# Attention scores from stacked high and low parts through DRAM, and routing spread over more steps in another PSUM bank

## The reference

```python
# layer 0, attention: q from layernorm(x), k and v from ctx
scores = einsum('bhqd,bhkd->bhqk', q, k) / sqrt(16)
out = einsum('bhqk,bhkd->bhqd', softmax(scores), v) @ W_O + b_O
x = x + tanh(g) * out
# layer 0, experts: top 2 of 8, relu, 256 -> 1024 -> 256, gates by softmax of the two
# layer 1, attention: the same with a causal mask and a key mask, no biases, no W_O
# layer 1, experts: top 2 of 8 by sparsemixer, silu(gate) * up, 256 -> 512 -> 256
```

## Time and profile before

| | |
|---|---|
| median of three runs | 1904.41 us (1901.04 to 1904.66) |
| the profiled execution | 1892.92 us |
| its span, first to last instruction | 1891.1 us |
| mean granted clock of TensorE | 0.920 of full |
| busy: PE, DVE, ACT, POOL | 88%, 64%, 63%, 42% |
| attention of layer 0, first to last transpose of probabilities | 47.2 to 453.4 us |
| experts of layer 0 | about 510 to 985 us |
| attention of layer 1, likewise | 1030.9 to 1428.0 us |
| experts of layer 1 | about 1485 to 1850 us |
| chain of work that ended last | PE 81%, DVE 8%, DMA 3%, issue 3%, POOL 2%, ACT 2% |

### The profile page before, as it was taken

The page is one execution under the profiler, slowest core; times in us unless marked ns, Lnnn a source line. Parts: engine busy times, 40 slices in busy tenths (PEclk is TensorE's granted clock), DMA queues, the critical chain, the costliest instruction groups (busy, mean ns, idle before and its releaser), DMA issues.

```text
span 1891.1 us, 36389 instructions
## 1 busy us (share of the span) xinstructions
PE 1672.7 (88%) x12444; PEld 1587.1 (84%) x12444; DVE 1210.5 (64%) x2859; ACT 1196.0 (63%) x2795; POOL 792.5 (42%) x877
## 2 busy tenths in 40 slices
PE   3999999998399999999975999999994599999990
PEld 2898888887399999999974998888884599999990
DVE  3465566654477777777756667767655566666655
ACT  2776566663188888888853766655562477777760
POOL 2123333323356666666652112323312366666650
PEclk9998899996599999999997999989896699999995
DMA  2112222112467777788742223322220577777758
GB/s 92 46 47 66 62 55 56 48 39 71 124 206 231 233 233 229 228 230 234 229 155 88 62 63 84 83 75 76 55 71 26 175 238 225 231 234 232 229 181 275
DMA packets 209513, 265.59 MB, mean 140 GB/s; under 512 B 28224, under 2 KB 155460, under 8 KB 209200
## 3 DMA queue, kind: packets, MB, share of 16 engines
q1 hardware_dynamic: 189840, 222.36, 40.8%
q0 software_dynamic: 13632, 35.13, 5.1%
q10 hardware_dynamic: 5856, 5.77, 1.0%
HBM read 202.89 MB, written 45.69 MB: 131 GB/s over the span
## 4 chain that ended last, share of the span: by engine, by line
PE 81%; DVE 8%; DMA 3%; issue 3%; POOL 2%; ACT 2%; SPq 1%; POOLq 0%; DVEq 0%; ACTq 0%
PE ps L363 19%; PE ps L365 19%; PE ps L364 19%; PE ps L484 10%; PE ps L383 6%; PE ps L494 2%; PE ps L465 2%; POOL xs_scr L1132 2%; PE ps L399 1%; DMA U<-ys_scr 1%; PE ps L415 1%; PE ps L458 1%; DVE X L1331 1%; DVE mx L912 1%; DMA xs_scr<-U,PI 1%
## 5 line engine op out<-in xcount | busy, mean ns | idle before, releaser
L1035 POOL TENSOR_TENSOR KXR<-U,KXR 128x1024 fp32r<-128x1024 f32 (+1 forms) x156 | 334.4, 2144 | 308.0 <-ACT KXR L645 307.2
L363 PE MATMUL ps<-QR,KXR 128*128 128x256 f32 x1248 | 355.1, 285 | 8.5 <-DVE QR L1039 8.5
L364 PE MATMUL ps<-QR,KXR 128*128 128x256 f32 x1248 | 354.7, 284 | 0.0
L365 PE MATMUL ps<-QR,KXR 128*128 128x256 f32 x1248 | 354.3, 284 | 0.0
L645 ACT ACTIVATE KXR<-U 128x1024 fp32r<-128x1024 f32 (+1 forms) x312 | 287.7, 949 | 78.0 <-PE ps L365 62.1
L555 ACT ACTIVATE U<-ps,mx 128x128 f32<-128x128 f32 x1024 | 293.9, 388 | 4.7 <-DVE mx L912 4.7
L484 PEld LDWEIGHTS ps<-VA,U 128*128 128x128 f32 x2048 | 275.8, 203 | 11.8 <-DVE U L901 1.2
L484 PE MATMUL ps<-VA,U 128*128 128x17 f32 x2048 | 264.7, 263 | 1.0 <-DVE U L901 1.0
L363 PEld LDWEIGHTS ps<-QR,KXR 128*128 128x128 f32 x1248 | 238.6, 191 | 9.7 <-DVE QR L1039 9.7
L364 PEld LDWEIGHTS ps<-QR,KXR 128*128 128x128 f32 x1248 | 238.6, 191 | 0.0
L365 PEld LDWEIGHTS ps<-QR,KXR 128*128 128x128 f32 x1248 | 238.3, 191 | 0.0
(11 more groups left out here) (190 smaller groups left out, 3949.2 us busy)
## 6 DMA issues: line engine op xcount, KB each, us to landing
U<-in_wpack SPq DMA_DIRECT2D x234, 512.0 KB, 4.1
U<-xs_scr SPq DMA_DIRECT2D x78, 257.0 KB, 4.4
U<-in_wpack SPq DMA_DIRECT2D x78, 256.0 KB, 3.6
KXR<-U SPq DMA_DIRECT2D x512, 32.0 KB, 2.0
U<-in_ctx_t SPq DMA_DIRECT2D x16, 512.0 KB, 4.1
U<-ys_scr SPq DMA_DIRECT2D x32, 256.0 KB, 3.0
U<-ys_scr SPq DMA_DIRECT2D x16, 512.0 KB, 10.2
XR<-in_L_ffn_b SPq DMA_DIRECT2D x39, 128.0 KB, 3.9
```

Source lines behind the costliest of these rows:

```text
L363: e.matmul(o, wh, xh, start=first, stop=False)
L364: e.matmul(o, wh, xl, start=False, stop=False)
L365: return e.matmul(o, wl, xh, start=False, stop=done)
L1035: e.tensor_tensor(w_cols(L, WL, n), w_raw(L, n), hi, ALU.subtract).then_inc(*l_w[n](L, i))
```

## The change

**Scores.** A pair of heads takes 32 rows, and three of them are stacked on 96 partitions: Q as high, low, high and K as high, high, low. One matmul over 96 rows gives all three products. With K's zeros kept only within a pair it has 256 columns for two heads, and a unit takes two of them (and two mask matmuls of 256 columns in layer 1). To stack, Q and K with their rests are written to a DRAM scratch (`qk_d`, 1 MB each per group) and read back for half a group at a time by nine transfers (`sp_stack`). `QR` becomes the stacked `QX`, two half groups deep, and `KX` likewise; both parts of Q and K of one group stand in `U1`.

**Order of projections.** XT, Q and K come a group earlier or closer together: `X0`, `Q0`, `K0`, `V0`. Layer norm, the loads of x and YL, and CT move ahead with them (a line of the diff each). The loop begins at -38.

**Routing** moves to bank `BK`, into more and closer steps; the rank matmuls' result is copied to `RK` at once (in `dve_rests`), and `dve_route` and `dve_rank2` fall into `dve_max`, `dve_index`, `dve_sel`, `dve_rank` and `dve_rows`. `ot` and `op` keep `BO_` for themselves.

**VectorE's order.** The maxima of unit `s + 3` come first in a step, ahead of `rec`, `ON` and the rests. Layer norm's and `XR`'s four batches are split over two steps.

```diff
-        self.lt = (self.e0 + 4, self.e0 + (6 if g < NG - 1 else 5))
-        self.e1 = self.e0 + (8 if g < NG - 2 else 7 if g < NG - 1 else 6)
-        self.d = (2, 4, 5) if g < NG - 2 else (1, 3, 4) if g < NG - 1 else (1, 2, 3)
+        late = g == NG - 1
+        self.lt = (self.e0 + 4, self.e0 + 5)
+        self.e1 = self.e0 + 6
+        (self.max, self.index, self.sel, self.gates, self.exp, self.gates2, self.rk, self.rank, self.rows, self.scatter) = (
+            self.e1 + k for k in ((1, 1, 1, 1, 1, 2, 2, 3, 3, 3) if late else (1, 2, 2, 3, 3, 4, 3, 4, 5, 6)))
-FIRST, LAST = -21, 146
+FIRST, LAST = -38, 147
+X0, Q0, K0, V0 = (-10, -9), (-8, -7), (-1, 0), (4, 11)
...
+        KX = KXR[:, :].rearrange("p (r c a n) -> p r c a n", r=2, c=8, a=2)
+        QX = QR[:, :].rearrange("p (r c n) -> p r c n", r=2, c=8)
...
                 if 0 <= s + 4 < NU:
-                    js = slice(j * 128, j * 128 + 128)
-                    kh, kl = (KX[:, b % 2, p, m, 4 * z:4 * z + 4, :].rearrange("p h k -> p (h k)") for p in range(2))
-                    ins = three(e, bank[:, :], (QR[:, g % 2, 0, m, js], QR[:, g % 2, 1, m, js]), (kh, kl), True, L == 0)
+                    js = slice((b % 2) * 128, (b % 2) * 128 + 128)
+                    for c in range(2):
+                        o, pk = bank[:, c * 256:(c + 1) * 256].rearrange("p (a k) -> p a k", a=2), 2 * (i % 4) + c
+                        ins = e.matmul(o, QX[0:96, r, pk, js], KX[0:96, r, pk, :, js], start=True, stop=L == 0)
+                        if L == 1:
+                            ins = e.matmul(o, IR[:, :], MK[:, g % 2, j:j + 1, :].to_broadcast([128, 2, 128]), start=False, stop=True)
...
+                if s == p.rk:
+                    w.wait_ge(*m_rk[k])
+                    e.tensor_copy(RK[:, :, 0:p.n], BK[:, 0:64].rearrange("p (z g e) -> p z g e", z=2, g=G)[:, :, 0:p.n]).then_inc(*v_rk(*k))
...
             for s in range(FIRST, LAST):
+                if 0 <= s + 3 < NU:
+                    i = s + 3
+                    w.wait_ge(*m_s[L, i])
+                    e.tensor_reduce(mx[:, i % 4], ...)
                 if (b := bat(s, 6)) is not None:
                 dve_rests(e, w, L, s - 1)
-                if 0 <= s + 3 < NU:
-                        if (g := grp(s, -3 + j)) is not None:
+                        if (g := grp(s, -19 + j)) is not None:
-                    if (g := grp(s, -2 + j)) is not None:
+                    if (g := grp(s, -18 + j)) is not None:
-                if (g := grp(s, 2)) is not None:
+                if (g := grp(s, -14)) is not None:
-                if (g := grp(s, 5)) is not None:
+                for n in range(2):
+                    if (g := grp(s, -12 + n)) is not None:
...
+        def sp_stack(e, w, L, h):
+            g, r, ns = h // 2, h % 2, slice((h % 2) * 256, (h % 2) * 256 + 256)
+            if h >= 2:
+                w.wait_ge(*m_s[L, 8 * (h - 2) + 7])
+            w.wait_ge(*d_qd[L, g])
+            for n in range(3):
+                src = qk_d[L][g, 0].rearrange("(c a) (z n) -> a z c n", c=8, z=2)[:, (0, 1, 0)[n], :, ns]
+                e.dma_start(QX[32 * n:32 * n + 32, r].bitcast(F32), src).then_inc(*d_q[r](L, h, n))
+            w.wait_ge(*d_kd[L, g])
+            for n in range(6):
+                q, a = n // 2, n % 2
+                src = qk_d[L][g, 1].rearrange("(c b a) (z n) -> b a z c n", c=8, b=2, z=2)[a, :, (0, 0, 1)[q], :, ns]
+                e.dma_start(KX[32 * q + 16 * a:32 * q + 16 * a + 16, r, :, a, :].bitcast(F32), src).then_inc(*d_k[r](L, h, n))
...
-                        if (g := grp(s, -5 + j)) is not None:
+                        if (g := grp(s, -21 + j)) is not None:
-                    for h in range(8):
-                        hs = slice(16 * h, 16 * h + 16)
-                        e.dma_start(KX[hs, v, :, :, h, :].rearrange("p z m k -> p (z m) k").bitcast(F32),
+                if (g := grp(s, Q0[1] + 1)) is not None:
+                    w.wait_ge(*v_q[L, g, 1])
+                    e.dma_start(qk_d[L][g, 0].rearrange("(m p) n -> p m n", m=2), U1[:, 2048:4096].rearrange("p (m n) -> p m n", m=2)).then_inc(*d_qd(L, g))
+                if (g := grp(s, K0[1] + 1)) is not None:
+                    w.wait_ge(*v_k[L, g, 1])
+                    e.dma_start(qk_d[L][g, 1].rearrange("(m p) n -> p m n", m=2), U1[:, 0:2048].rearrange("p (m n) -> p m n", m=2)).then_inc(*d_kd(L, g))
+                for n in range(2):
+                    if (g := grp(s, (3, 12)[n])) is not None:
+                        sp_stack(e, w, L, 2 * g + n)
```

More of the change, by code:

```diff
@@ L313, in w_raw, with uses_bk @@
             return U1[:, n * 1024:n * 1024 + NFs[L] * D // 2]
-        def bank7(L):
+        def uses_bk(L):
             out = []
             for s in range(FIRST, LAST):
[L319 to L324, removed]
+                for name, at, empty in (("xt", X0, v_xt), ("q", Q0, v_q), ("k", K0, v_k), ("v", V0, a_v)):
+                    for n in range(2):
+                        if (g := grp(s, at[n])) is not None:
+                            out.append(((name, g, n), empty[L, g, n]))
                 for p in PARTS:
@@ L975, in dve_attention @@
                             w.wait_ge(*a_ct[L, NG - 1])
-                        for j in range(p.lo, p.hi):
-                            ins = e.tensor_scalar(xr(p.g)[:, 0, j, 0:D], X[:, p.g * G + j], mv[:, 1, j, 0:1], rs[:, 1, 1, j:j + 1], ALU.subtract, ALU.mult)
-                        ins.then_inc(*v_xr(*k))
-                    if s == p.e1 + p.d[0]:
-                        dve_route(e, w, L, p)
+                        elif p.lo == 0 and p.g:
+                            w.wait_ge(*d_sc[(p.g - 1) % 2][L, p.g - 1, 0, 1, G - 1])
+                            w.wait_ge(*m_lt[L, p.g - 1, 0, 1])
+                        mid = (p.lo + p.hi) // 2
+                        for j in (range(p.lo, mid), range(mid, p.hi))[s - p.e0 - 2]:
+                            ins = e.tensor_scalar(xr(p.g)[:, 0, j, 0:D], X[:, p.g * G + j], mv[:, 1, j, 0:1], rs[:, 1, 1, j:j + 1], ALU.subtract, ALU.mult)
+                        if s == p.e0 + 3:
+                            ins.then_inc(*v_xr(*k))
+                    if s == p.max:
+                        dve_max(e, w, L, p)
+                    if s == p.index:
+                        dve_index(e, w, L, p)
+                    if s == p.sel:
+                        dve_sel(e, w, L, p)
+                    if s == p.gates:
                         dve_gates(e, w, L, p)
-                    if s == p.e1 + p.d[1]:
+                    if s == p.gates2:
                         dve_gates2(e, w, L, p)
-                    if s == p.e1 + p.d[2]:
-                        dve_rank2(e, w, L, p)
+                    if s == p.rank:
+                        dve_rank(e, w, L, p)
+                    if s == p.rows:
+                        dve_rows(e, w, L, p)
                 if (b := bat(s, 11)) is not None:
@@ L1215, in sp_attention @@
             for s in range(FIRST, LAST):
-                if (g := grp(s, -4)) is not None:
+                if (g := grp(s, -8)) is not None:
                     if g >= 2:
@@ L1224, in sp_attention @@
                                     .rearrange("p (b s) -> p b s", b=G)).then_inc(*d_mi(g))
-                if L == 0 and (g := grp(s, -8)) is not None and g:
+                if L == 0 and (g := grp(s, -22)) is not None and g:
                     sp_load_x(e, g)
```

278 lines of the change are left out of this document (131 added, 147 removed).

## The result

The changed kernel is a little slower: 1922.31 us median of 20 runs (1897.08 to 1932.76) against 1905.16 us for the kernel before (1900.40 to 1917.64), a ratio of 1.0058, 95% interval 1.0034 to 1.0082. Ratios here leave out the executions that fell in a slower state of the chip, so they are not the quotients of the medians. Later the same two kernels, run again, gave 1.0089 (1.0054 to 1.0125). I had forecast 1881 us, faster.

What follows compares the result with a forecast made beforehand. TensorE was taken to bound the attention groups. Steady-state savings of 71 us, +50 us before the first units and -2 us in layer 0's tail gave -23 us: 1881 us on the median's scale, range 1832 to 1926.

Steps and rivals of the forecast that it cites:

- Scores, 0.45 us a unit: Score matmuls of each unit: two of 256 columns instead of three of 512 save 0.45 us, bounds 0.13 to 0.54.
- Clock of layer 0's routing groups: Layer 0's four routing groups: mean clock 0.89 (before 0.93), 3 us idle each, 196 us against 214.8.
- the clock holds: Rival: routing groups at 0.95 with 2 us idle take 45.3 us, whole kernel 1831 us; chance 0.20.
- Clock of layer 1's routing groups: Layer 1's four routing groups: mean clock 0.90 (before 0.94), 4.5 us idle each, 200 us against 212.5.
- the formula: Group time: full-clock work divided by 1 - 0.465f, f being the share of time at low clock, plus idle time.
- Last groups: Last two groups of each layer: 84 us against 98.7 in layer 0, 81 against 94.2 in layer 1.
- DRAM round trip hidden in steady state: Q and K through DRAM: 6.4 us write plus 8.6 us half-group read fit within 27 us of lead.
- Start, layer 0: Before layer 0's first unit: more serial projections put first scores at 61.5 against 41.44 us; +18 us after 2 back.
- Layer 1 with the tail: Start of layer 1, +32 us from serial projections and YL additions, with layer 0's tail at 2 us less.
- Waits on PI gone: Layer 0's output projection no longer waits for a bank held until PI is written: 13.7 us over six waits.
- Maxima first costs nothing: VectorE's new order costs nothing by itself and keeps exponentials from waiting for value matmuls.
- the clock giving way: Rival: thin steps and new stalls put routing groups at 0.80 and 54.7 us, whole kernel 1928 us; chance 0.18.

Runs made afterwards that it cites:

- r_after: The changed kernel itself, unchanged, run again beside later runs: 1918.87 us, 1.0089 of the kernel before.
- r_e1: e1 once more, unchanged, on another chip: 1871.28 us, 0.9811 of the kernel before.
- e1: Changed kernel with YL's loads, additions and the bn_stats behind them four steps earlier in layer 1: 1875.38 us, 0.9860 of the kernel before.
- e4: Changed kernel with XT and Q of group 1 moved behind the first scores in both layers: 1907.54 us, 1.0021 of the kernel before.
- e13: e9 with the maxima back behind the reciprocals, ON and the rests, as in the kernel before: 1889.68 us, 0.9864 of the kernel before.
- e9: e1 with one added 480-column matmul ahead of each batch's router matmuls, both layers: 1852.50 us, 0.9713 of the kernel before; 0.9966 on a fourth chip.
- e3: Changed kernel with score matmuls issued three times over in each layer's last sixteen units: 1930.71 us, 1.0153 of the kernel before.
- e8: Changed kernel with e1's and e4's edits plus two added 512-column matmuls per step of each layer's last group: 1957.22 us, 1.0122 of the kernel before.

## Why the prediction was wrong, point by point

- **Scores, 0.45 us a unit**: right. With the clock at 1.00 a routing group of layer 0 of the changed kernel (r_after) was 42.40 us with 41.73 of TensorE work; I had 41.3.

```profile
202.69:245.09 42.40, 41.73 (x342) 39.68 (x342) 31.24 (x102) 33.69 (x96) 18.17 (x39) 1.00 0.72 175
```

- **Clock of layer 0's routing groups**: 0.89 forecast, 0.95 measured, and idle time 0.7 us a group, not 3. Four groups 177.5 instead of 196. Both terms were too dark here; in layer 0 it was the rival "the clock holds" (0.95, 45.3 us a group) that came out. The first two took 82.9 us (forecast 85.4), with one miss inside: the second of them now has a router step, so that its TensorE work is 41.33 us (r_e1, at full clock), not 38.3.
- **Clock of layer 1's routing groups, the step that failed**: 0.90 forecast, 0.79 measured. The idle time was about right (15.3 / 4 = 3.8 us against 4.5), and so was the formula: 41.3 / (1 - 0.465 x 0.42) + 3.8 = 55.1 us, measured 55.6. At 0.90 it gave 50. The four groups are 22.5 us over the forecast, all of it clock. The first two, put at 86, took 108.5; with the wait gone (e1) they take 82.5 and the four 198.2, which is what I had forecast (86 and 200). I had written that K's rest stands behind two additions, and priced it once, for the start. It stands there in each group, and I took its idle time, some 3 us, as the whole price: the 17 to 20 us at 0.50 behind it I had put at nothing.
- **Last groups**: forecast 84 and 81 us for the last two, measured 93.2 and 91.9. That is 9 and 11 us more. The clock did not dip, it stayed at 0.50 (in r_after, layer 0's last group had a mean of 0.80, and the last two took 76.3). The missing row was a plain step without projections at the low clock; none of the kernel before has one with thin scores. What decides whether the clock comes back there stays open.
- **DRAM round trip hidden in steady state**: right; no score matmul waited for `KX` or `QX` after the first unit. The landing times were 5.0 us for 1 MB (forecast 6.4), and write and stack together took 15.2 us in e4 (forecast 6.4 + 8.6). But the transfers were not free for others: ctx landed in 8.5 us, where the kernel before had it in 4.1, and YL's loads stood behind the stack. I priced the stack for its own reader and not for those queued behind it on SyncE, though I counted its 18 issues.
- **Start, layer 0**: +18 forecast, +27.8 measured. Q of group 0 was written at 35.3 (forecast 35.2), K at 45.5 (43), Q of group 1 at 65.3 (60), first scores at 68.0 (61.5). Then K of group 1 stood ahead of the first transpose and cost 2.7 more (72.3 to 75.0), which I had left out. The 2 us that I took off at the end did not come back. Layer 1 with the tail: +30 forecast, +30.2 measured.
- **Waits on PI gone**: right. **Maxima first costs nothing**: true, but by e13 it gains something, perhaps 1%, and I gave it nothing.
- **Rivals.** The one that came nearest in time, the clock giving way (1928 us, 18%), gave its clock to both layers alike, and layer 0 went the other way. Its border, a mean of 0.85 in routing groups, is crossed in layer 1 alone. In layer 1 it came out, with its price (54.7 us a group, measured 55.6). It named thin steps and new stalls as the cause: by e1 the stalls at YL were the larger part (50 us in six groups), and by e9 the router steps took a further 13.6 us of four. That its total of 1928 lies near 1922 is luck, since layer 0 and the last groups went other ways.
- **The Trainium skill's rule** (TensorE: Matmul & The Clock Gate, Part 4: PE-mode transpose), that transposes don't count as activity like matmuls, fits the last groups, where transposes went on and the clock stayed at 0.50, but no run here takes the transposes alone away. The same page's Part 1 (The HAM clock gate) says that the clock is low when TensorE has been idle and high when it has been busy. By the trace that is not enough: TensorE was busy 54.29 of 54.29 us at 0.50.

## What to carry to other kernels

When a change makes matmuls fewer or thinner, forecast the clock with its waits: for each wait that the change puts ahead of a projection, price the idle time and then the low-clock steps behind it, up to the next projection (here 17 to 20 us). A wait that is moved past another engine's queue must be looked up in every group, not only at the start. And measure on more than one chip before trusting a gain that hangs on the clock: 2.9% on one was 0.3% on another.

## What the runs showed of the hardware

- A fully busy TensorE can stay at 0.50: 53 to 65 us in the last groups of the changed kernel, e3 and e8, through steps of transposes, 256-column scores, and 17-column value matmuls, in some even with 1024 more columns a step.
- The clock fell behind sixteen router matmuls of 8 columns. An added matmul of 480 columns ahead of each batch's four (0.9 us a group) kept it up there: 13.6 us less over four groups of layer 1. In the last group it did so in three profiles of seven, and in the kernel before it gained nothing (1.0029).
- After waits of 2.4 to 3.2 us on a projection the clock was at 0.50 for 17 to 20 us, in five groups of five.
- The last group of layer 0 stood at 0.50 or at 0.80 in two executions of the same code.
- TensorE stops of 1 to 1.8 us with no releaser appear in the same code on some chips and not on others, beside 1 MB of loads.
- A 256 KB load of YL landed in 6.3 us behind the stack on SyncE's queue, in 4.2 from GpSimd's, and in 3.1 when issued four steps earlier.
- e9 is the best version run on two chips: 0.9713 (0.9634 to 0.9791) of the kernel before on one, 0.9966 (0.9934 to 0.9997) on the other.
